# Moving the projection fills, their evacuations and the output work to other steps of an attention pipeline

## The reference, cut to what matters

```python
# x: (4, 1024, 512), cond: (4, 512), 16 heads of 32, all float32
def sln(h, w):                       # conditioned layer norm
    ln = (h - mean) / sqrt(var + 1e-5) * ln_g + ln_b
    return (w @ Wg.T + bg) * ln + (w @ Wb.T + bb)
h = sln(x, cond)
q, k, v = split(h @ Wqkv.T + bqkv)   # 16 heads
att = softmax(q @ k.T) / sqrt(512)   # per head, 1024 x 1024
out = concat_heads(att @ v) @ Wp.T + bp
h1 = out + x
result = sln(h1, cond) + h1
```

## Time and profile before

| | us |
|---|---|
| median of 3 runs | 1650.23 (1648.33 to 1650.9) |
| the profiled execution, its own time | 1652.41 |
| its span, first to last instruction | 1650.7 |
| PE busy | 1448.1 (88%) |
| POOL busy | 1027.9 (62%) |
| DVE busy | 924.6 (56%) |
| ACT busy | 713.7 (43%) |
| mean granted clock of TensorE | 0.931 of full speed |

### The profile page before, as it was taken

One profiled execution on the slowest core, in us unless ns is written; L12 is line 12 of the kernel. 1 busy time (PEld: TensorE's weight loads), 2 busy tenths in 40 slices (PEclk: granted clock), 3 DMA queues, 4 the chain that ended last, 5 costly groups with the idle time before them and its releaser, 6 DMA issues.

```text
span 1650.7 us, 35294 instructions
## 1 busy us (share of the span) xinstructions
PE 1448.1 (88%) x10804; PEld 913.7 (55%) x10804; DVE 924.6 (56%) x1633; ACT 713.7 (43%) x1370; POOL 1027.9 (62%) x779
## 2 busy tenths in 40 slices
PE   6989999999999999989999989999888888889434
PEld 4887656565656556565656656565454545454223
DVE  4347666666665555555656555655565656565035
ACT  3222454545454444444544444454545454545200
POOL 2442656464647675867768585847676767676647
PEclk9999999999999999999989999999898989899766
DMA  6668333333344243343425334253323232321142
GB/s 208 174 185 199 106 91 104 91 103 90 99 107 136 69 136 94 111 115 108 138 79 136 83 109 123 76 142 87 91 82 87 80 90 77 90 77 47 34 119 84
DMA packets 219737, 175.61 MB, mean 106 GB/s; under 512 B 106741, under 2 KB 189685, under 8 KB 219673
## 3 DMA queue, kind: packets, MB, share of 16 engines
q1 hardware_dynamic: 217368, 167.46, 37.7%
q0 software_dynamic: 2304, 7.34, 1.2%
HBM read 114.87 MB, written 59.05 MB: 105 GB/s over the span
## 4 chain that ended last, share of the span: by engine, by line
PE 38%; POOL 25%; issue 20%; POOLq 4%; DVE 4%; DMA 4%; SPq 4%; ACT 1%; DVEq 1%; ACTq 0%
POOL p L1250 14%; PE ps_o L692 7%; PE ps_a L661 7%; PE ps_w L625 7%; PE ps_st L675 5%; PE ps_s L705 4%; PE ps_st L625 3%; PE ps_w L568 2%; POOLq L1172 2%; POOL y_t L1227 2%; POOL y_t L1229 2%; POOL oT_s L1203 2%; POOL y_t L1221 2%; DVE half_max L1048 2%; SPq L419 1%
## 5 line engine op out<-in xcount | busy, mean ns | idle before, releaser
L1048 DVE TENSOR_REDUCE half_max<-ps_a 128x1 f32<-128x512 f32 x1024 | 675.9, 687 | 389.7 <-PE ps_a L661 378.0
L1250 POOL TENSOR_TENSOR p<-p 128x1024 f32<-128x1024 f32 x256 | 604.8, 2383 | 442.9 <-PE ps_o L692 442.1
L860 ACT ACTIVATE p<-ps_st 128x512 f32<-128x512 f32 x1024 | 585.9, 600 | 593.4 <-PE ps_st L675 532.3
L661 PE MATMUL ps_a<-k_stack,q_stack 96*128 96x512 f32 x1024 | 466.3, 461 | 39.5 <-DVEq L1060 14.1
L675 PE MATMUL ps_st<-q_stack,k_stack 98*128 98x512 f32 x1024 | 434.3, 426 | 45.0 <-DMA q_stack<-max_rows 26.9
L661 PEld LDWEIGHTS ps_a<-k_stack,q_stack 96*128 96x128 f32 x1024 | 198.4, 195 | 230.5 <-DVE half_max L1048 159.7
L692 PE MATMUL ps_o<-p,v_head 128*32 128x256 f32 x4096 | 254.9, 391 | 0.0
L675 PEld LDWEIGHTS ps_st<-q_stack,k_stack 98*128 98x128 f32 x1024 | 203.0, 199 | 82.8 <-issue 29.7
L692 PEld LDWEIGHTS ps_o<-p,v_head 128*32 128x32 f32 x4096 | 136.3, 114 | 104.8 <-issue 20.1
L705 PE MATMUL ps_s<-p,root_s 128*1 128x256 f32 x2048 | 152.0, 413 | 19.8 <-POOL p L1250 19.8
L625 PEld LDWEIGHTS ps_w<-hT_s,wqkv_s 128*128 128x128 f32 x1056 | 149.1, 191 | 33.7 <-DVE qkT_s L972 13.0
(11 more groups left out here) (98 smaller groups left out, 989.5 us busy)
## 6 DMA issues: line engine op xcount, KB each, us to landing
qk_scratch<-qkT_s SPq DMA_DIRECT2D x108, 256.0 KB, 2.4
q_stack<-qk_scratch SPq DMA_DIRECT2D x192, 128.0 KB, 2.7
k_stack<-qk_scratch SPq DMA_DIRECT2D x192, 128.0 KB, 2.9
x_tile<-in_x SPq DMA_DIRECT2D x32, 256.0 KB, 5.2
gq_s<-gain_bias_scratch SPq DMA_DIRECT2D x16, 512.0 KB, 4.6
v_scratch<-v_parts SPq DMA_DIRECT2D x32, 256.0 KB, 3.1
v_head<-v_scratch SPq DMA_DIRECT2D x64, 128.0 KB, 2.1
att_scratch<-o_stage SPq DMA_DIRECT2D x256, 32.0 KB, 1.5
```

Source lines behind the costliest of these rows:

```text
L661: pe.matmul(ps_a[:, parity, :], q_stack[0:96, s, t * 128:(t + 1) * 128], k_stack[0:96, s, half * 512:(half + 1) * 512], start=True, stop=T ...
L860: nc.scalar.activation(p32[:, k, e * 512:(e + 1) * 512], ps_st[:, ST_BANK[2 * k + e], :], ACT.Exp).then_inc(exp_done, 1)
L1048: V.tensor_reduce(half_max[:, s % 2, item:item + 1], ps_a[:, parity, :], AX.X, ALU.max).then_inc(a_used, 1)
L1250: G.tensor_tensor(p32[:, slot, :], p32[:, slot - 2, :], p32[:, slot, :], ALU.add).then_inc(pair_added, 1)
```

## The change

Fills get a table of pieces, `PROJECTED`, by step and place (start, middle or end of the step), in units of a sixth of a part. A fill f from 3 to 8 now has a third of its products at the end of step 4f - 7 (the step after a burst) and the rest in four pieces over the next two steps, so that it ends in the step before the next burst. Fill 2 has its first half at the end of step 2 and its second in step 3; fill 9 its first half at the end of step 29 and its second in step 30. Fills 8 and 9 are those of the output. Fill 0 is at the start of step 0, ahead of its other products, fill 1 at its end. Fills 2 to 8 are evacuated in the burst step (`EVACUATED`: 4, 8, ..., 28), fill 9 in step 31; fills 0 and 1 in steps 0 and 1, on ACT ahead of that step's exponentials. DVE's other statistics move: input tile 1 from step 9 to 7, output tiles from 25 and 29 to 28 and 31. On POOL the residual moves to steps 15 and 16, the scaling of the attention output to 16 and 19, the low parts to 20 and 23, tile 0's scale and finish both to step 31, and tile 1's to steps 3 and 4 of the next iteration (`finish_late`). For that POOL's first iteration with outs is written out ahead of the loop, and the last pair's is done after the loop. SP stores q and k one step after the evacuation (steps 5, 9, 13, 17) and v at 22 and 26. No instruction's size changes and none is added, apart from that.

```diff
-PAIR_STAGE = {0: (0, 0), 2: (1, 0), 4: (2, 0), 5: (2, 1), 7: (3, 0), 8: (3, 1), 10: (4, 0), 11: (4, 1),
-              13: (5, 0), 14: (5, 1), 16: (6, 0), 17: (6, 1), 19: (7, 0), 20: (7, 1)}
-OUT_STAGE = {21: (0, 1), 22: (0, 2), 25: (1, 1), 26: (1, 2)}
-PIECES = (range(0, 2), range(2, 6))
-LN_STEP = {5: 0, 9: 1}
-OUT_STATS_STEP = {25: 0, 29: 1}
+PROJECTED = {(0, "start"): [(0, 0, 0, 6)], (0, "end"): [(1, 0, 0, 6)],
+             (2, "end"): [(2, 0, 0, 6)], (3, "mid"): [(2, 1, 0, 3)], (3, "end"): [(2, 1, 3, 6)]}
+for _fill in range(3, 10):
+    PROJECTED[4 * _fill - 7, "end"] = [(_fill, 0, 0, 4)]
+    PROJECTED[4 * _fill - 6, "mid"] = [(_fill, 0, 4, 6)]
+    PROJECTED[4 * _fill - 6, "end"] = [(_fill, 1, 0, 2)]
+    PROJECTED[4 * _fill - 5, "mid"] = [(_fill, 1, 2, 4)]
+    PROJECTED[4 * _fill - 5, "end"] = [(_fill, 1, 4, 6)]
+PROJECTED[29, "end"] = [(9, 0, 0, 6)]
+PROJECTED[30, "mid"] = [(9, 1, 0, 3)]
+PROJECTED[30, "end"] = [(9, 1, 3, 6)]
+del PROJECTED[31, "mid"], PROJECTED[31, "end"]
+EVACUATED = {0: 0, 1: 1, 2: 4, 3: 8, 4: 12, 5: 16, 6: 20, 7: 24, 8: 28, 9: 31}
+LN_STEP = {5: 0, 7: 1}
+OUT_STATS_STEP = {28: 0, 31: 1}
...
-RESIDUAL_STEP = {3: 0, 4: 1}
+LATE_STEP = {3: 0, 4: 1}
...
-OUT_NORM_STEP = {15: 0, 16: 1}
-OUT_LOW_STEP = {19: 0, 20: 1}
-OUT_SCALE_STEP = {27: 0, 31: 1}
-OUT_FINISH_STEP = {28: 0, 31: 1}
+RESIDUAL_STEP = {15: 0, 16: 1}
+OUT_NORM_STEP = {16: 0, 19: 1}
+OUT_LOW_STEP = {20: 0, 23: 1}
+OUT_SCALE_STEP = {31: 0}
+OUT_FINISH_STEP = {31: 0}
-V_STORE_STEP = {22: 0, 24: 1}
+V_STORE_STEP = {22: 0, 26: 1}
...
-OUT_HIGH_STEP = {17: 0, 18: 1}
+OUT_HIGH_STEP = {18: 0, 20: 1}
...
+                        project("start")
                         for use in uses[:1]:
                             a_item(*use)
...
                             turned_scores(*after, 0)
-                        piece(step - 1, 1)
+                        project("mid")
...
-                        piece(step, 0)
+                        project("end")
...
+                    if fill in (0, 1):
+                        tile_high(i + LEAD, fill)
                     exps(i, step)
...
-                    if tiles and fill is not None and fill < 6:
+                    if fill in (2, 3, 4, 5):
                         tile_high(i + LEAD, fill)
...
-                        if outs and step - 1 in OUT_STAGE and OUT_STAGE[step - 1][1] == 2:
-                            out_sum(pair, OUT_STAGE[step - 1][0])
+                        if outs and fill in (8, 9):
+                            out_sum(pair, fill - 8)
...
+            def finish_late(pair, part):
+
+                count = 10 * pair + 5 + ONE
+                if part == 0:
+                    out_scale(pair, 1, count)
+                else:
+                    out_finish(pair, 1, count)
...
+                    if outs and late and step in LATE_STEP:
+                        finish_late(pair - 1, LATE_STEP[step])
...
+            for part in range(2):
+                finish_late(END - 1, part)
             residual(END, 0)
```

More of the change, by code:

```diff
@@ L277, in evacuated @@
             return stage[0] if stage and (stage[1] == 1 or stage[0] < 2) else None
+        TAKEN_AT = {step: fill for fill, step in EVACUATED.items()}
         W_BANK = [ps_st[:, 0, :], ps_st[:, 1, :], ps_st[:, 2, :], ps_s[:]]
@@ L514, in iteration @@
                         if tiles:
-                            for fill in range(2, 6):
-                                if evacuated(PAIR_STAGE, step - 2) == fill:
-                                    store_rows(i + LEAD, fill)
+                            fill = TAKEN_AT.get(step - 1)
+                            if fill in (2, 3, 4, 5):
+                                store_rows(i + LEAD, fill)
                             if step in V_STORE_STEP:
@@ L596, in _, with stage @@
                     mm.then_inc(mod_ready, 1)
-            def stage(pair, fill, part, lead=False, piece=None):
+            def stage(pair, fill, part, lead=False, lo=0, hi=6):
                 bank = bank_of(fill, lead)
[L602 to L606, removed]
+                if part == 0 and lo == 0:
                     before = LEAD_BEFORE[fill] if lead else fill - 1
@@ L616, in stage @@
                     return
-                if fill == 2 and part == 0 and piece != 1:
+                if fill == 2 and part == 0 and lo == 0:
                     pe.wait_ge(tile_ev, 8 * pair + 2 + PAIR_BEFORE)
@@ L622, in stage @@
                     w, chunk = (fill - 2) // 2, 2 * (fill % 2) + part
-                    for n in [n for p in passes for n in (2 * p, 2 * p + 1)]:
+                    for n in range(2 * lo, 2 * hi):
                         d, (lp, rp) = n // 3, SPLIT[n % 3]
@@ L733, in iteration, with project @@
                         uses = ring_uses(i, s, k, last)
[L735 to L749, removed]
+                        def project(at):
+                            for fill, part, lo, hi in PROJECTED.get((step, at), ()):
+                                if fill < 8 and tiles:
+                                    if fill == 0 and outs:
+                                        pe.wait_ge(out_summed, 2 * pair + ONE)
+                                    stage(i + LEAD, fill, part, lo=lo, hi=hi)
+                                elif fill >= 8 and outs:
+                                    if (fill, part, lo) == (8, 0, 0):
+                                        pe.wait_ge(tile_ev, 8 * (i + LEAD + 1 if tiles else PAIRS) + PAIR_BEFORE)
+                                    out_part(pair, fill - 8, part, lo=lo, hi=hi)
+                        project("start")
                         for use in uses[:1]:
@@ L792, in _ @@
                 for a in range(2):
-                    for k in (1, 2):
-                        out_part(m, a, k, end=True)
+                    for part in range(2):
+                        out_part(m, a, part, end=True)
         @block.scalar
@@ L876, in iteration @@
                     s, k = step // 8, step % 8
-                    fill = evacuated(PAIR_STAGE, step)
+                    fill = TAKEN_AT.get(step) if tiles else None
                     if first and step == 2:
@@ L1107, in iteration @@
                         split = None if last and s == 3 else (i + (s + 1) // 4, (s + 1) % 4)
-                        if tiles and evacuated(PAIR_STAGE, step - 1) in (2, 3, 4, 5):
-                            take(i + LEAD, evacuated(PAIR_STAGE, step - 1))
+                        fill = TAKEN_AT.get(step)
                         ring(uses[:1])
+                        if tiles and fill in (0, 1):
+                            take(i + LEAD, fill)
                         ring(uses[1:])
@@ L1113, in iteration @@
                             max_negated(*split, A_LEAD + 17 * (4 * i + s) + 7)
-                        fill = evacuated(PAIR_STAGE, step)
-                        if tiles and fill in (0, 1, 6, 7):
+                        if tiles and fill in range(2, 8):
                             take(i + LEAD, fill)
@@ L1263, in _, with iteration @@
                 norm(LEAD, a)
-            def iteration(i, tiles, norms, outs, first=False):
+            def finish_late(pair, part):
[4 more added lines that the diff above has]
+                    out_finish(pair, 1, count)
+            def iteration(i, tiles, norms, outs, first=False, late=True):
                 pair = i - FIRST_OUTS
@@ L1295, in _ @@
                 iteration(i, True, True, False)
-            with pool.Fori(FIRST_OUTS, LAST_TILES - 1) as i:
+            iteration(FIRST_OUTS, True, True, True, late=False)
+            with pool.Fori(FIRST_OUTS + 1, LAST_TILES - 1) as i:
                 iteration(i, True, True, True)
```

13 lines of the change are left out of this document (6 added, 7 removed).

## The result

The changed kernel takes 1570.59 us, the median of four runs (1561.7 to 1574.54), against 1650.26 before: a ratio of 0.9512, 95% interval 0.9464 to 0.9559. The forecast was 1592, with a range of 1573 to 1622. The direction was right, the gain 80 us in place of 58, and the time lies just under the range.

A forecast was written before the change was run, and what follows sets the result against it. PE was taken to bound the kernel, with waits for banks and a lowered clock. Gains of 44.0 (tiles and outs), 6.2 (tiles alone), 1, 5.4 (outs alone) and 2 sum to 58.6 us off 1650.2: 1592, range 1573 to 1622.

The forecast's parts named there:

- One fill a round, emptied under the burst: Fills 3 to 9: the wait for the bank goes, DVE's pass (0.69 or some 0.9 us) just hidden beside a burst.
- A round cannot be shorter than the rows with one fill.: Rounds (burst to burst) with one fill take at least the profiled one-fill times, 9.8 to 10.7 us.
- My rows of 10.67, 9.80 and 10.35: Profiled rounds taken as prices: one q/k fill starting at k = 4, one v-shaped fill at k = 0 and k = 4.
- R1 to R6 without R3: Rounds between the iteration's first and last, tiles and outs, skipping step 12's: forecast 10.7, 10.1, 9.8, 10.35 and 9.8 us.
- R0: Round from step 0's burst, tiles and outs: 10.1 + 0.35 + 0.85 + 0.5 = 11.8 us.
- R7: Round from step 28's burst, tiles and outs: 10.35 + 1.5 + 1.1 + 0.35 = 13.3 us.
- The clock term: With tiles and outs, half speed behind the waits of R7 loses 1.5 us an iteration; bounds nothing and 3.2.
- Rival A: The clock stays up, as the waits of R7 may not trip it: 1580 us, chance 0.14.
- the first wait: At the start of step 0 with outs, PE's transposes of fill 0 wait 1.5 us for DVE's sum of fill 9.
- the second: Step 1's second score product waits 1.1 us for its bank, as ACT takes the transposes before step 0's exponentials.
- The row in R3: In the round from step 12's burst, PE waits 1.1 us for the row of maxima; bounds 0 and 3.5.
- POOL with tiles costs nothing: R7 and R0 hold 12.15 us of POOL work each; the 0.4 us excess of R0 is absorbed in the next round.

The follow-up runs named there:

- Experiment 5: The changed kernel with fills 2 to 8 evacuated one step later, behind the burst, and output tile 0's statistics moved along: 1715.69 us, ratio 1.0384.
- Experiment 1: The changed kernel with the last piece of fills 3 to 8 joined to the piece in the middle of that step: 1586.87 us, ratio 0.9617.
- experiment 9: The changed kernel run again, unedited: median 1567.53 us of six runs, ratio 0.9506.
- Experiment 3: The changed kernel with fill 0 behind the burst of step 0 and fill 1 at the end of step 1, each evacuated a step later: 1565.09 us.
- Experiment 4: The changed kernel with POOL's output work placed as in the kernel before, none carried into the next iteration: 1607.91 us, ratio 0.9736.
- experiment 6: The kernel before with POOL's part of the change alone, its fills, evacuations and statistics as before: 1635.41 us, ratio 0.9908.

## Why the prediction was right and wrong

**One fill a round, emptied under the burst: right, and the largest part.** No fill from 3 to 9 waits for its bank any more, as the page's groups of q and k products and of output products say with their last figure, the idle time before them (9.5 and 11.8 us before):

```profile
L633 PE MATMUL ps_w<-hT_s,wqkv_s 128*128 128x256 f32 x1056 | 159.2, 283 | 0.0
...
L580 PE MATMUL ps_w<-wp_s,oT_s 128*128 128x512 f32 x288 | 82.9, 396 | 0.0
```

Experiment 5 puts the price of the opposite at 145 us. DVE's three passes do fit beside a burst.

**The step that failed: "A round cannot be shorter than the rows with one fill."** It can. My rows of 10.67, 9.80 and 10.35 had one fill each, but cut otherwise: nothing stood at the end of the step ahead of the burst, and the burst step's own products then waited for DVE. The end of the first pair in the earlier trace rows, in the trace of the kernel before:

```profile
360.06 0.39 PE L675 MATMUL ps_st<-q_stack,k_stack 98*128 98x512 f32 x1
...
360.53 0.19 PEld L661 LDWEIGHTS ps_a<-k_stack,q_stack 96*128 96x128 f32 x1 [0.51 <-DVE half_max L1048]
360.53 0.50 PE L661 MATMUL ps_a<-k_stack,q_stack 96*128 96x512 f32 x1
```

I took the price of a round's content from rounds with another order. It measured 10.1, 9.5, 9.4 and 10.0 for my 10.7, 10.1, 9.8 and 10.35. In R1 to R6 without R3 that is 2.2 us an iteration with tiles and outs (10.1 + 9.5 + 9.4 + 10.0 + 9.5 = 48.5 for 50.75), and in R1 to R5 with tiles alone 2.5 us (49.2 for 51.65). Experiment 1 gave 0.35 of it back a round by moving one piece. The unread sign was in the trace: the products of the burst step start 0.34 to 0.47 apart, not 0.24. In this execution the iterations with tiles and outs are 20 us under the forecast: 16 from these rounds, 9 from the clock, 5 from R0 and 1 from R7, less 11 that R3 took back.

**The clock term was mis-sized.** I had 1.5 us an iteration behind the waits of R7; the stage's clock is 0.99, and of the six edges with such waits only that behind iteration 4 has half speed (R7 13.8 us for 12.7 to 13.0). In the profile of experiment 9 there are three (R7 13.8 to 14.0). Rival A was right in the one and half right in the other. The Trainium skill's page "TensorE: Matmul & The Clock Gate", section "HAM oscillation — how this bites in real kernels", asks for a stream without idle gaps; the clocks here (by stage 0.99 with one fill a round and 0.92 with outs alone; over the whole run 0.949, and 0.915 in experiment 5) agree with it as a tendency. The page's own case has longer gaps than the waits here, and whether half speed follows a given one of these the last section shows to be open.

**R0 was 0.8 too long** (11.0 for 11.8). Most of it is the first error again: I built R0 on 10.1 for a plain q/k round, and R2, which is one, measured 9.5. The product that waits for the bank starts 0.88 after its neighbour, so this cost 0.64 for my 0.85; the next products add some 0.4 for my 0.5.

**The edge: the first wait right, the second too long.** PE waited 1.47 us for the output sum, as forecast. The score product behind ACT's evacuation cost 0.63 for my 1.1, which is why R7 is 12.9 and not 13.3. Experiment 3 shows besides that only 1.1 us an iteration come back when fill 0 goes elsewhere.

**The row in R3 went against me:** 2.4 us of wait for 1.1. The queue of SP was costed right (9.2 us, and the store of fill 4 ahead), its start not: SP began 6.8 us ahead of the burst's end, not 7.5, and the row left 3.6 after it, not 2.5 (my own terms give 9.2 + 1.0 - 7.5 = 2.7). This hid part of the first error: 12.8 for 11.8.

**POOL with tiles costs nothing: right.** From 462 to 1062 us PE never waits for POOL's additions; its waits there are the row of maxima (17.0 us in seven), the output sum (8.6 in six), the exponentials (6.3) and DVE's copy of the maxima (9.3). Experiment 4 shows that the spreading is what makes it so, though 11 of its us with tiles stand in R3, behind a wait that is not POOL's. The parts don't add up: fills without POOL's tables give 42 us (1650 to 1608), POOL's tables without the fills 14, both together 80; half speed that comes or goes with a mere shift is in each of these differences. With outs alone I had R1 at 11.6 and R2 at 7.8, measured 12.5 and mostly 9.3 to 9.5, as the wait for POOL's additions there is followed by half speed.

In iteration 6 the errors are R0 -0.8, the five plain rounds -2.2, R3 +1.0, R7 -0.4 and the clock -1.5: 3.9 us off the forecast's 89.2, or 85.3, against the 85.2 measured. That the parts fit so well is for this iteration and this execution, the fastest of its set; the median is 9 us longer. Why the time of the same kernel varies by 0.8% stays partly open. The longest executions have the lowest mean clock (0.941 at 1574.5 for 0.949 at 1561.7; in experiment 9, 0.938 at 1578.8 for 0.948 at 1565.1), and the profiles show R3 and the edge with and without half speed behind much the same waits, which would account for it; but only one execution of each set was profiled.

## What to carry to other kernels

Price a stretch by a row with the same order of work, not only the same amount: look at the spacing of the bound engine's instructions at the point that the change touches. Empty a single-buffered bank while its writer is busy with something else for long enough; here one step later cost more than the whole change brought. And read an issuing queue as a resource: six transfers that nothing was waiting for yet stood ahead of the one that the next head needed, and putting them behind it was worth some 50 us, where the whole change brought 80.

## What the runs showed of the hardware

The same wait of TensorE may or may not be followed by half speed. Behind 1.71 us for the same bank the granted clock was 0.50 in the kernel before and 1.00 in experiment 6; behind 2.40 us for the row of maxima it was full in the changed kernel, behind 2.33 half in experiment 3 and behind 2.60 half in experiment 4. A stretch at half speed cost 1.4 to 1.7 us of its round in these places. So the length of such a wait alone does not say whether this second price is paid. Nor is it drawn anew each time: within one execution the outcome mostly repeats (R5 is 14.8 us in all six of iterations 4 to 9 of the kernel before and 13.2 in all of them in experiment 6). What decides it no run here shows. An edit that only shifts a wait in time can so seem to gain or lose some 10 us: R5 in experiment 6 gained 9, R3 in experiments 3 and 4 lost 7.5 and 11.
